# Row statistics, normalised rows and softmax scaling on VectorE: one tile of a chunk to a quarter of a slot

## Chip, core and metric

The kernel runs on one core of a Trainium2 chip. The metric is the device time of one execution in microseconds (us). TensorE does the matrix products and transposes, VectorE, ScalarE and POOL the elementwise work and reductions, and SyncE (SP) issues most of the transfers. The engines run their own instructions in order and meet at semaphores.

## The reference, cut to what matters

`x` has 2048 tokens of width 256, `ctx` has 1601. Layer 0 is a cross attention with 16 heads of width 16, then a mixture of 8 experts (the best one is taken); layer 1 is an attention over a masked window of 256 context rows, then a routing of every token to 64 slots, whose state is updated once from all tokens.

```python
x = x + xcond0(layernorm(x), ctx, ctx)          # 16 heads, softmax over 1601 keys, plus Wo
x = x + experts(layernorm(x))                   # router: softmax, top 1 of 8; y * weight
x = x + tanh(cat([align @ enc, n]) @ W_c.T)     # n = layernorm(x); align = softmax(mask(n W_a enc)) * gauss
x = x + slots(layernorm(x))                     # h = gelu(n w1); logits = h w2; alpha = softmax of the top 8 of 64;
                                                # slot update from alpha^T n over ALL tokens; out = alpha @ values
def layernorm(x): return (x - mean(x)) / sqrt(var(x) + 1e-5)
```

(The sums with `x` and the layer norms stand around the layers in the whole program; the lines above are shortened.)

## The kernel before

The tokens are four chunks of 512, and a chunk is four tiles of 128 rows (`TT` = 4). The main loop takes a chunk's attention in 52 slots: four head groups times 13 blocks of 128 keys. A slot has four quarters, one for each head of the group, so a chunk has 208 quarters.

In each quarter TensorE makes one score product (line 1189, two buffers, `ps_e`), ScalarE takes its exponential (line 750), and at the end of a slot TensorE multiplies the probabilities of the slot before with the values (line 985). The softmax needs the maximum of each row of scores beforehand. So TensorE also makes the scores of the next head group a first time (line 901, `max_unit`) in pieces of 401 columns into a ring of three buffers (`RING` = 3), and VectorE reduces each piece to a maximum (line 1335, `take_max`). There are 1, 2, 1, 1 of these products in the four quarters of most slots. Product u waits until piece u - 3 has been reduced. In the last third of chunk 3 there are no more such products, since there is no chunk after it.

All that follows the attention of chunk c, from the output projection to the slots, runs in the quarters of chunk c + 1: the functions `behind(c)` of TensorE, VectorE, ScalarE and POOL. They are generators. A `yield q` tells that what follows is due in quarter q, and each engine's `go_on` runs what is due after its own attention work of that quarter (on VectorE after the maxima of the quarter and, in the first quarter of a slot's third key block, after `normalise`). The jobs of the last chunk run after the main loop without quarters, in the same order on each engine.

The quarter of each job is worked out by `places` from the table `JOBS` (name, job it follows, least distance in quarters, quarters that it holds its buffer). The TensorE jobs share two banks in turn; a job needs the bank of the one but one before it to be read out. The order of the banks counts two fixed kinds of job too, the turned attention output ("o", quarters 6, 58, 110, 162) and the turned maxima ("m", 45, 97, 149, 201), so a job can be pushed past them. `AT[name]` is the quarter.

The layer norms go as follows (t1 before the experts, t2 before the window, t3 before the slots). VectorE computes the statistics of each tile (`bn_stats`, line 1417) and their aggregate (`bn_aggr`, line 1421). POOL adds epsilon and takes the power -0.5 (lines 597 and 599, `rsqrt`). VectorE waits for it (`rstd_ready`), writes four tiles of `xn` (line 1327, `normal`), and TensorE transposes them (`turned`, jobs t1a, t1b and so on; line 1030), waiting for `xn_ready` at t1a, t2a and t3a. ScalarE copies the transposes to `xnT` (line 760).

In the window softmax, VectorE adds the mask, takes the row maximum (line 1490), negates it (line 1492), ScalarE takes the exponentials of the four tiles with their sums (line 793), VectorE divides (`reciprocal`, then line 1504 for each tile) and TensorE transposes (aTa, aTb). In the slots, VectorE computes `alpha` (lines 1528 to 1556) from the logits, and TensorE multiplies it with `xn` (job slots, line 1171).

SP stores `x` after the third sum (`x3`) and loads the next chunk's `x` into the same tile once the third `xn` of the chunk is written.

Of the kernel before, what the change touches and what calls it, by code (L numbers as in the profile page):

```python
# [12 lines left out]
ALU = mybir.AluOpType  # L13
# [4 lines left out]
T, D = 2048, 256  # L18
# [4 lines left out]
NC = T // CT  # L23
TT = CT // P
# [5 lines left out]
NE = 2 * TT * NX // 4  # L30
# [91 lines left out]
def units_at(k, h):  # L122
# [5 lines left out]
O_AT = [HG * (ST * g + 1) + 2 for g in range(NG)]  # L128
M_AT = [HG * k + 1 for k in range(SLOTS) if max_end(k - 1) is not None]

JOBS = [("ota", None, 10, 3), ("otb", "ota", 2, 3), ("y0", "otb", 3, 3), ("y1", "y0", 2, 3), ("t1a", "y1", 11, 3),
        ("t1b", "t1a", 2, 3), ("router", "t1b", 3, 2), ("e0", "router", 5, 6)]
JOBS += [(f"e{i}", f"e{i - 1}", 4, 6) for i in range(1, 4)] + [("gateT", "e3", 3, 3), ("e4", "gateT", 1, 6)]
JOBS += [(f"e{i}", f"e{i - 1}", 4, 6) for i in range(5, NE)]
JOBS += [("gb0", f"e{NE - 1}", 4, 4), ("gb1", "gb0", 2, 4), ("t2a", "gb1", 11, 3), ("t2b", "t2a", 2, 3),
         ("score0", "t2b", 3, 3), ("score1", "score0", 2, 3), ("aTa", "score1", 13, 3), ("aTb", "aTa", 2, 3),
         ("z0", "aTb", 3, 9), ("z1", "z0", 8, 9), ("t3a", "z1", 20, 3), ("t3b", "t3a", 2, 3), ("h", "t3b", 3, 5),
         ("logits", "h", 6, 2), ("slots", "logits", 14, 6), ("alphaT", "slots", 4, 3)]


def places():

    fixed = sorted([(q, q + 3) for q in O_AT] + [(q, q + 2) for q in M_AT])
    ring, at = [(0, 0), (0, 0)], {}
    for name, after, lag, hold in JOBS:
        q = at[after] + lag if after else lag
        while True:
            while fixed and fixed[0][0] < q:
                ring.append(fixed.pop(0))
            q = max(q, ring[-2][1])  # L150
            if not fixed or fixed[0][0] >= q and ring[-1][1] <= fixed[0][0]:
                break
            q = max(q, fixed[0][0] + 1)
        at[name] = q
        ring.append((q, q + hold))
    return at


AT = places()
# [38 lines left out]
def build(nc, io):  # L198
    with ExitStack() as ctx:
        def sb(name, shape, dt=F32):  # L200
            return ctx.enter_context(nc.sbuf_tensor(name, shape, dt))
# [4 lines left out]
        def sem(name):  # L206
            return ctx.enter_context(nc.semaphore(name))
# [9 lines left out]
        xres = sb("xres", [P, TT, D])  # L217
# [18 lines left out]
        alphaT = alphaT_raw[0:NS + 1, :]  # L236
        xa = sb("xa", [P, TT, D])
# [6 lines left out]
        xb = sb("xb", [P, TT, D])  # L244
        xn = sb("xn", [P, TT, D + 1])
# [47 lines left out]
        mv = sb("mv", [P, TT, 2])  # L293
        var_e = sb("var_e", [P, TT])
        rstd = sb("rstd", [P, TT])
# [18 lines left out]
        at = [0]  # L314
# [51 lines left out]
        s = {n: sem(n) for n in names}  # L366
# [10 lines left out]
        def bank(job, c):  # L377
            return ps_m[:, RING + JOB[job, c] % 2, :]
# [284 lines left out]
        def _(act):  # L663
# [79 lines left out]
            for _, now in BESIDE:  # L743
                step(*now)
# [508 lines left out]
        def _(dve):  # L1253
# [67 lines left out]
                    last = dve.bn_aggr(mv[:, t, :], bst[:, t, :])  # L1321
                last.then_inc(s["var_ready"], 1)

            def normal(src, n):
                dve.wait_ge(s["rstd_ready"], n)
                for t in range(TT):
                    last = dve.tensor_scalar(xn[:, t, 0:D], src[:, t, :], mv[:, t, 0:1], rstd[:, t:t + 1],  # L1327
                                             ALU.subtract, ALU.mult)
                last.then_inc(s["xn_ready"], 1)

            def take_max(u, n1):
                t, h, q = u // (QUARTERS * HG), (u // QUARTERS) % HG, u % QUARTERS
                dve.wait_ge(s["max_ready"], UNITS * n1 + u + 1)
# [77 lines left out]
            def spread_stats(src, at):  # L1411

                dve.drain()
                for t in range(TT):
                    if t % 2 == 0:
                        yield at + t // 2
                    dve.bn_stats(bst[:, t, :], src[:, t, :])
                yield at + 2
                dve.drain()
                for t in range(TT):  # L1420
                    last = dve.bn_aggr(mv[:, t, :], bst[:, t, :])  # L1421
                last.then_inc(s["var_ready"], 1)

            def behind(c):

# [5 lines left out]
                yield AT["y1"] + 3  # L1431
                yield from spread_stats(xa, AT["y1"] + 3)
                yield AT["t1a"] - 4
                normal(xa, NC + 3 * c + 1)

                yield AT["router"] + 1
                wait_filled(dve, "router", c)
# [27 lines left out]
                for i in range(NE):  # L1465
                    t, j = i // 4, i % 4
                    for e in (2 * j, 2 * j + 1):
                        yield AT[f"e{i}"] + 4 + e % 2
                        dve.drain()
                        if e % 2 == 0:  # L1470
                            wait_filled(dve, f"e{i}", c)
                        last = dve.scalar_tensor_tensor(out=xb[:, t, :], in0=bank(f"e{i}", c)[:, D * (e % 2):D * (e % 2) + D],  # L1472
                                                        scalar=hot8[:, t, e:e + 1], in1=(xb if e else xa)[:, t, :],
                                                        op0=ALU.mult, op1=ALU.add)
# [4 lines left out]
                    take_sum(xb[:, 2 * i:2 * i + 2, :], xb[:, 2 * i:2 * i + 2, :], f"gb{i}", c)  # L1479
                yield from spread_stats(xb, AT["gb1"] + 4)  # L1480
                yield AT["t2a"] - 4
                normal(xb, NC + 3 * c + 2)

                for i in range(2):
                    yield AT[f"score{i}"] + 2
                    at = slice(2 * i, 2 * i + 2)
# [12 lines left out]
                dve.reciprocal(st4[:, 6, :], rowsum[:])  # L1499
                dve.drain()  # L1500
                for t in range(TT):
                    if t == 2:
                        yield AT["score1"] + 9
                    last = dve.tensor_scalar(work[:, t, :], work2[:, t, :], st4[:, 6, t:t + 1], None, ALU.mult)
                last.then_inc(s["a_ready"], 1)
                if c == NC - 1:
# [13 lines left out]
                                           work[:, 2 * i:2 * i + 2, :], ALU.add)  # L1520
                x3.then_inc(s["x3_ready"], 1)
                yield from spread_stats(xres, AT["z1"] + 11)
                yield AT["t3a"] - 3
                normal(xres, NC + 3 * c + 3)

                yield AT["logits"] + 1
                wait_filled(dve, "logits", c)
# [165 lines left out]
```

## Time and profile before

| what | before |
|---|---|
| median of 3 runs | 1118.73 us (1114.81 to 1122.76) |
| the profiled execution | 1120.53 us |
| its span, first to last instruction | 1118.8 us |
| TensorE busy | 1008.3 us, 90% |
| VectorE busy | 742.0 us, 66% |
| ScalarE busy | 573.4 us, 51% |
| POOL busy | 62.3 us, 6% |
| mean granted TensorE clock | 0.960 of full speed |

The span is 1.7 us shorter than the execution's own time. Busy TensorE (PE) is not TensorE at its peak, since matmuls are pipelined and their ends are modelled. Lines such as L1335 are lines of the kernel. Quarters are found in the trace by counting the products of line 1189, of which each quarter has one: chunk 1 begins at 264.88 us, and its quarter 20 at 286.23.

### The profile page before, as it was taken

Reading aid. Unit: us, or ns where it says so; the run is one execution under the profiler, and the core shown is the slowest. Engines: PE = TensorE matmul, PEld = TensorE weight load, DVE = VectorE, ACT = ScalarE, POOL = GpSimd, SP = SyncE. Lnnn points to the kernel's source line nnn. Section 1 sums busy time; section 2 is a strip of 40 time slices with the busy share of each in tenths; the row PEclk is TensorE's granted clock in tenths of the full one; section 3 lists DMA queues with packets and bytes.
Section 4 is the critical chain, followed back from the end, with each engine's and each line's share of the span. In section 5 each row is a group of like instructions: output and inputs, shape, how many; then the busy total and the mean of one; then the engine's idle time right before and its main releaser. Section 6 shows DMA issues by size and latency. Waiting matters only on the chain.

```text
span 1118.8 us, 13600 instructions
## 1 busy us (share of the span) xinstructions
PE 1008.3 (90%) x4825; PEld 403.5 (36%) x4825; DVE 742.0 (66%) x1681; ACT 573.4 (51%) x1056; POOL 62.3 (6%) x85
## 2 busy tenths in 40 slices
PE   6788999999889989989989989898999989889887
PEld 3443223223333334423333334323333333244634
DVE  4578877877667777776667776777677672125343
ACT  3455676676445456665445456655444467620220
POOL 3341000000000000000000000001000000000000
PEclk9899999999999989999899999999999899699998
DMA  7925600001000000001000000010000001040022
GB/s 183 193 70 95 121 11 15 6 10 34 1 16 1 15 0 13 4 6 48 1 15 1 16 1 15 1 53 1 15 1 1 1 1 39 1 119 0 1 95 75
DMA packets 33773, 36.06 MB, mean 32 GB/s; under 512 B 6639, under 2 KB 30365, under 8 KB 33445
## 3 DMA queue, kind: packets, MB, share of 16 engines
q1 hardware_dynamic: 32384, 34.04, 12.1%
q10 hardware_dynamic: 1242, 0.90, 0.6%
q8 instruction: 38, 0.62, 0.2%
q0 software_dynamic: 80, 0.26, 0.1%
q14 instruction: 29, 0.24, 0.1%
HBM read 21.42 MB, written 7.35 MB: 26 GB/s over the span
## 4 chain that ended last, share of the span: by engine, by line
issue 52%; PE 28%; DVE 9%; DMA 4%; ACT 2%; POOL 2%; DVEq 2%; SPq 1%; POOLq 0%; ACTq 0%
PE ps_e L1189 7%; PE ps_o L985 7%; PE ps_m L901 6%; DVE mx L1335 4%; PE ps_e L861 2%; DMA xres<-in_x 1%; SPq L471 1%; POOL rstd L599 1%; DMA q_stack<-probs 1%; POOL xres L650 1%; ACT probs L750 1%; DVE xn L1327 1%; PE ps_m L1133 1%; PE ps_m L1136 1%; PE ps_m L1248 1%
## 5 line engine op out<-in xcount | busy, mean ns | idle before, releaser
L1335 DVE TENSOR_REDUCE mx<-ps_m 128x1 f32<-128x401 f32 x1024 | 539.4, 569 | 212.3 <-PE ps_m L901 204.1
L750 ACT ACTIVATE probs<-ps_e 128x512 f32<-128x512 f32 (+1 forms) x832 | 472.2, 597 | 362.3 <-PE ps_e L1189 360.9
L901 PE MATMUL ps_m<-k_stack,q_stack 99*128 99x401 bf16 x1024 | 319.1, 343 | 34.4 <-DVE mx L1335 29.7
L1189 PE MATMUL ps_e<-q_stack,k_stack 101*128 101x512 bf16 (+1 forms) x832 | 329.2, 398 | 11.8 <-ACT probs L750 9.1
L985 PE MATMUL ps_o<-probs,v_heads 128*32 128x512 f32 (+1 forms) x1664 | 231.7, 630 | 0.0
L1189 PEld LDWEIGHTS ps_e<-q_stack,k_stack 101*128 101x128 bf16 (+1 forms) x832 | 82.5, 100 | 314.0 <-ACT probs L750 215.5
L901 PEld LDWEIGHTS ps_m<-k_stack,q_stack 99*128 99x128 bf16 x1024 | 102.3, 100 | 150.8 <-DVE mx L1335 90.9
L1083 PE MATMUL ps_m<-expert_w,xnT 128*128 128x512 f32 x256 | 129.1, 605 | 16.3 <-DVE xb L1472 16.3
L1472 DVE SCALAR_TENSOR_TENSOR xb<-ps_m,hot,xb 128x256 f32<-128x256 f32 x112 | 54.2, 484 | 18.1 <-PE ps_m L1083 8.9
L1083 PEld LDWEIGHTS ps_m<-expert_w,xnT 128*128 128x128 f32 x256 | 46.7, 193 | 47.4 <-DVE xb L1472 24.7
L985 PEld LDWEIGHTS ps_o<-probs,v_heads 128*32 128x32 f32 (+1 forms) x1664 | 33.4, 110 | 66.6 <-issue 56.9
L597 POOL TENSOR_TENSOR var_e<-mv,eps 128x4 f32<-128x4 f32 x16 | 3.2, 199 | 679.3 <-DVE mv L1421 676.2
L760 ACT COPY xnT<-ps_m 128x512 f32<-128x512 f32 x24 | 13.8, 587 | 46.5 <-PE ps_m L1030 46.5
L1005 PE MATMUL ps_m<-wc,ident 128*128 128x512 f32 x64 | 30.9, 624 | 0.8 <-ACT alphaT L819 0.8
L650 POOL TENSOR_TENSOR xres<-xres,bo 128x1024 f32<-128x1024 f32 x4 | 9.4, 2350 | 266.9 <-DMA xres<-in_x 266.9
L861 PE MATMUL ps_e<-xnT,expert_w 128*128 128x512 f32 x32 | 18.8, 677 | 4.4 <-issue 3.1
L1133 PE MATMUL ps_m<-win_v,work 128*128 128x256 f32 x64 | 19.6, 399 | 2.3 <-ACT work L760 2.3
L1519 DVE TENSOR_TENSOR xres<-xb,work 128x512 f32<-128x512 f32 x8 | 5.5, 687 | 22.4 <-ACT work L803 22.4
L1136 PE MATMUL ps_m<-wc,xnT 128*128 128x256 f32 x64 | 19.3, 395 | 0.0
L1030 PE MATMUL ps_m<-ident,xn 128*128 128x128 f32 x96 | 17.8, 283 | 1.3 <-DVE xn L1327 1.2
L677 ACT ACTIVATE work<-ps_e,cond 128x512 f32<-128x512 f32 (+1 forms) x11 | 7.2, 653 | 22.2 <-PE ps_e L861 22.2
L1040 PE MATMUL ps_m<-win_k,xnT 128*128 128x256 f32 x64 | 16.2, 383 | 2.2 <-issue 1.4
(241 smaller groups left out, 636.9 us busy)
## 6 DMA issues: line engine op xcount, KB each, us to landing
q_stack<-q_parts SPq DMA_DIRECT2D x78, 64.0 KB, 2.6
expert_w<-in_expert_wT SPq DMA_DIRECT2D x2, 1024.0 KB, 13.2
xres<-in_x SPq DMA_DIRECT2D x4, 512.0 KB, 3.8
x<-xres SPq DMA_DIRECT2D x4, 512.0 KB, 3.2
probs<-x SPq DMA_DIRECT2D x1, 2048.0 KB, 8.4
out<-probs SPq DMA_DIRECT2D x4, 512.0 KB, 3.0
k_stack<-alphaT SPq DMA_DIRECT2D x10, 200.1 KB, 7.7
probs<-in_ctxT SPq DMA_DIRECT2D x3, 512.0 KB, 7.8
```

The source lines that it names most:

```text
L650: pool.tensor_tensor(xres[:], xres[:], bo0[:].unsqueeze(1).broadcast_to((P, TT, D)), ALU.add)\
L750: act.activation(probs[0:n, k % 2, h, :], ps_e[h % 2][0:n, :], ACT.Exp).then_inc(s["exp_done"], 1)
L861: mm = pe.matmul(ps_e[b % 2][:, 0:n], wqkv[:, w, k, P * m:P * m + P], src[:, k, at_col:at_col + n], start=(k == 0), stop=(k == KT - 1))
L901: pe.matmul(ps_m[:, (UNITS * n1 + u) % RING, 0:SPLIT], qst[0:MAX_ROW, g, h, P * t:P * t + P], kst[0:MAX_ROW, HG * g + h, QUARTER_START[q]: ...
L985: mm = pe.matmul(ps_o[32 * h:32 * h + 32, :], v_sb[0:n, st, HG * g + h, :], probs[0:n, k % 2, h, :], start=(st == 0), stop=(st == ST - 1))
L1005: pe.matmul(out, ident[:], wc[:, 0:KT, :], start=True, stop=True)
L1083: mm = pe.matmul(bank(name, c), xnT[:, k, P * t:P * t + P], expert_w[:, k, CT * j:CT * j + CT], start=(k == 0), stop=(k == KT - 1))
L1133: pe.matmul(o, aT[:, k, tok:tok + P], win_v[:, k, :], start=(k == 0), stop=False)
L1136: mm = pe.matmul(o, xnT[:, k, tok:tok + P], wc[:, KT + k, :], start=False, stop=(k == KT - 1))
L1189: pe.matmul(ps_e[h % 2][0:n, :], kst[0:ROWS, HG * g + h, P * st:P * st + n], qst[0:ROWS, g, h, :], start=True, stop=True).then_inc(s["qk_r ...
L1335: dve.tensor_reduce(mx[:, q, col:col + 1], ps_m[:, (UNITS * n1 + u) % RING, 0:SPLIT], AX.X, ALU.max)\
L1472: last = dve.scalar_tensor_tensor(out=xb[:, t, :], in0=bank(f"e{i}", c)[:, D * (e % 2):D * (e % 2) + D], scalar=hot8[:, t, e:e + 1], in1=( ...
```

## The change

The statistics of tile t are due in quarter `at + t` (before: two tiles in `at`, two in `at + 1`), the aggregate in `at + 4` (before `at + 2`). `normal` is replaced by `spread_normal`: it waits for `rstd` once, then writes the tile t in quarter `at + t`, where all four were written in one quarter. The softmax scaling of tile t is due in `AT["score1"] + 8 + t` (before two in + 8, two in + 9). In `JOBS`, t1a and t2a follow their predecessors by 12 quarters instead of 11, slots follows logits by 12 instead of 14, and alphaT follows slots by 3 instead of 4. For t3 the first tile comes at `AT["t3a"] - 4` instead of - 3.

```diff
-JOBS = [("ota", None, 10, 3), ("otb", "ota", 2, 3), ("y0", "otb", 3, 3), ("y1", "y0", 2, 3), ("t1a", "y1", 11, 3),
+JOBS = [("ota", None, 10, 3), ("otb", "ota", 2, 3), ("y0", "otb", 3, 3), ("y1", "y0", 2, 3), ("t1a", "y1", 12, 3),
...
-JOBS += [("gb0", f"e{NE - 1}", 4, 4), ("gb1", "gb0", 2, 4), ("t2a", "gb1", 11, 3), ("t2b", "t2a", 2, 3),
+JOBS += [("gb0", f"e{NE - 1}", 4, 4), ("gb1", "gb0", 2, 4), ("t2a", "gb1", 12, 3), ("t2b", "t2a", 2, 3),
...
-         ("logits", "h", 6, 2), ("slots", "logits", 14, 6), ("alphaT", "slots", 4, 3)]
+         ("logits", "h", 6, 2), ("slots", "logits", 12, 6), ("alphaT", "slots", 3, 3)]
...
-            def normal(src, n):
-                dve.wait_ge(s["rstd_ready"], n)
-                for t in range(TT):
-                    last = dve.tensor_scalar(xn[:, t, 0:D], src[:, t, :], mv[:, t, 0:1], rstd[:, t:t + 1],
-                                             ALU.subtract, ALU.mult)
-                last.then_inc(s["xn_ready"], 1)
...
                 for t in range(TT):
-                    if t % 2 == 0:
-                        yield at + t // 2
+                    yield at + t
                     dve.bn_stats(bst[:, t, :], src[:, t, :])
-                yield at + 2
+                yield at + 4
                 dve.drain()
                 for t in range(TT):
                     last = dve.bn_aggr(mv[:, t, :], bst[:, t, :])
                 last.then_inc(s["var_ready"], 1)
+
+            def spread_normal(src, n, at):
+
+                dve.wait_ge(s["rstd_ready"], n)
+                for t in range(TT):
+                    yield at + t
+                    last = dve.tensor_scalar(xn[:, t, 0:D], src[:, t, :], mv[:, t, 0:1], rstd[:, t:t + 1],
+                                             ALU.subtract, ALU.mult)
+                last.then_inc(s["xn_ready"], 1)
...
                 yield AT["t1a"] - 4
-                normal(xa, NC + 3 * c + 1)
+                yield from spread_normal(xa, NC + 3 * c + 1, AT["t1a"] - 4)
...
                 yield AT["t2a"] - 4
-                normal(xb, NC + 3 * c + 2)
+                yield from spread_normal(xb, NC + 3 * c + 2, AT["t2a"] - 4)
...
                 for t in range(TT):
-                    if t == 2:
-                        yield AT["score1"] + 9
+                    yield AT["score1"] + 8 + t
                     last = dve.tensor_scalar(work[:, t, :], work2[:, t, :], st4[:, 6, t:t + 1], None, ALU.mult)
...
-                yield AT["t3a"] - 3
-                normal(xres, NC + 3 * c + 3)
+                yield AT["t3a"] - 4
+                yield from spread_normal(xres, NC + 3 * c + 3, AT["t3a"] - 4)
```

Worked out by `places` from the two tables, the quarters are:

| job | before | after | | job | before | after |
|---|---|---|---|---|---|---|
| ota, otb, y0, y1 | 10, 12, 15, 17 | the same | | t2a, t2b | 125, 127 | 127, 129 |
| t1a, t1b | 28, 30 | 29, 31 | | score0, score1 | 130, 132 | 132, 134 |
| router | 33 | 34 | | aTa, aTb | 145, 147 | 147, 150 |
| e0, e1, e2, e3 | 38, 42, 48, 52 | 39, 43, 49, 53 | | z0, z1 | 150, 158 | 153, 161 |
| gateT, e4 | 55, 58 | 59, 61 | | t3a, t3b | 178, 180 | 181, 183 |
| e5 to e12, every 4 | 64 to 92 | 65 to 93 | | h, logits | 183, 189 | 186, 192 |
| e13, e14, e15 | 98, 102, 106 | 99, 103, 107 | | slots | 203 | 204 |
| gb0, gb1 | 112, 114 | 113, 115 | | alphaT | 207 | 207 |

Due quarters on VectorE at the three layer norms (first and last statistics, aggregate, first and last tile, then TensorE's transposes): t1 before 20, 21, 22, 24, 24, 28 and after 20, 23, 24, 25, 28, 29; t2 before 118, 119, 120, 121, 121, 125 and after 119, 122, 123, 123, 126, 127; t3 before 169, 170, 171, 175, 175, 178 and after 172, 175, 176, 177, 180, 181. Beside that the gateT job now comes after the "o" job at 58, and aTb after the "m" job at 149, which changes which bank they take.

## Rows read from the trace of the kernel before

**Rows 1.** The page, part 1: busy us, share of the span, instructions

```profile
PE 1008.3 (90%) x4825; PEld 403.5 (36%) x4825; DVE 742.0 (66%) x1681; ACT 573.4 (51%) x1056; POOL 62.3 (6%) x85
```

**Rows 2.** Busy us (instructions) by chunk (1 and 3): engines, clock, DMA, GB/s

```profile
264.88:505.32 240.44, 219.61 (x1125) 85.05 (x1121) 176.02 (x392) 133.04 (x243) 5.98 (x7) 0.98 0.04 11
...
748.44:982.14 233.70, 212.34 (x1034) 78.40 (x1030) 135.35 (x310) 131.15 (x241) 8.32 (x8) 0.93 0.04 12
```

**Rows 3.** TensorE's waits in chunk 1: us in total, times, longest

```profile
PE ps_m L901 <- DVE mx L1335: 9.8, 18, 1.8
PE ps_m L1083 <- DVE xb L1472: 5.1, 4, 1.6
PE ps_e L1189 <- ACT probs L750: 1.8, 5, 0.8
PE ps_m L1040 <- issue: 0.9, 2, 0.5
...
PE ps_m L1161 <- ACT hT L811: 0.5, 1, 0.5
```

**Rows 4.** Timeline around t1 in chunk 1: start us, us, what [idle before, releaser]

```profile
286.23 0.39 PE L1189 MATMUL ps_e<-q_stack,k_stack 101*128 101x512 bf16 x1
...
292.28 1.38 DVE L1327 TENSOR_SCALAR xn<-xa,mv,rstd 128x256 f32<-128x256 f32 x4 [0.53 <-POOL rstd L599]
...
296.88 0.38 PE L1189 MATMUL ps_e<-q_stack,k_stack 101*128 101x512 bf16 x1
```

**Rows 5.** TensorE's waits for maxima in chunk 1: around t1, t2, t3

```profile
PE ps_m L901 <- DVE mx L1335: 2.7, 3, 1.8
...
PE ps_m L901 <- DVE mx L1335: 2.0, 4, 0.8
...
PE ps_m L901 <- DVE mx L1335: 1.8, 4, 0.5
```

**Rows 6.** Timeline around t2 in chunk 1, VectorE and TensorE

```profile
409.54 0.38 DVE L1421 BATCH_NORM_AGGREGATE mv<-bst 128x2 f32<-128x6 f32 x4
...
411.39 1.38 DVE L1327 TENSOR_SCALAR xn<-xb,mv,rstd 128x256 f32<-128x256 f32 x4 [0.52 <-POOL rstd L599]
...
412.68 3.46 DVE L1335 TENSOR_REDUCE mx<-ps_m 128x1 f32<-128x401 f32 x7
...
414.59 0.39 PE L1030 MATMUL ps_m<-ident,xn 128*128 128x128 f32 x2
414.81 0.38 PE L1189 MATMUL ps_e<-q_stack,k_stack 101*128 101x512 bf16 x1
...
415.20 0.38 PE L1030 MATMUL ps_m<-ident,xn 128*128 128x128 f32 x2
...
416.51 0.39 PE L1189 MATMUL ps_e<-q_stack,k_stack 101*128 101x512 bf16 x1
```

**Rows 7.** Timeline around gb0 in chunk 1, TensorE and VectorE

```profile
396.08 0.67 PE L1099 MATMUL ps_m<-expert_b_tiles,gateT 32*128 32x256 f32 x2 [0.47 <-DVE xb L1472]
396.52 0.25 DVE L1400 RECIPROCAL z_inv<-ps_m 128x16 f32<-128x16 f32 x1
...
396.85 0.42 DVE L1403 TENSOR_TENSOR attn_chunk<-ps_m,z_inv 128x256 f32<-128x256 f32 x1
```

**Rows 8.** Timeline around the score scaling in chunk 1, TensorE

```profile
431.60 0.39 PE L1189 MATMUL ps_e<-q_stack,k_stack 101*128 101x512 bf16 x1 [0.46 <-ACT probs L750]
```

**Rows 9.** Timeline around slots in chunk 1, VectorE and TensorE

```profile
497.14 0.43 DVE L1556 TENSOR_TENSOR work<-work,st 128x256 f32<-128x256 f32 x1
...
498.38 0.65 PE L1171 MATMUL ps_m<-xn,work 128*64 128x257 f32 x2
```

**Rows 10.** Stretches around t1's gap in chunks 1 and 2, as above

```profile
290.00:298.00 8.00, 5.84 (x38) 2.61 (x34) 6.86 (x19) 4.02 (x8) 1.22 (x2) 1.00 0.00 0
530.00:538.00 8.00, 5.84 (x28) 1.89 (x25) 5.82 (x17) 2.94 (x6) 1.22 (x2) 0.84 0.00 0
```

**Rows 11.** VectorE: max line, chunk 1; busy us, mean ns | idle

```profile
L1335 DVE TENSOR_REDUCE mx<-ps_m 128x1 f32<-128x401 f32 x256 | 136.8, 569 | 56.6 <-PE ps_m L901 54.7
```

## The prediction

> **What bounds the kernel.** I read the page's busy table first: TensorE is busy 1008.3 of the 1118.8 us [rows 1]. That alone does not say that it works all the time, so I cut the main loop at its four chunks [rows 2]. Chunk 1, with all jobs of chunk 0 beside its own attention, takes 240.4 us. Its list of TensorE's waits [rows 3] gives 9.8 us on VectorE's maxima, 1.8 us on ScalarE's exponentials and small ones on single jobs. So TensorE sets the pace, VectorE holds it up in bursts, and the change is about these bursts. It acts in chunks 1 to 3. Chunk 0 has no such jobs, and after chunk 3 there is no slot left to spread over: there the same instructions stand in the same order on each engine, so I add nothing for the end.
>
> How a burst costs TensorE time is seen in the stretch around t1a in chunk 1 [rows 4]. VectorE waits 0.53 us for POOL's rstd, then writes four tiles of xn in one go (1.38 us). Behind them stand the maxima. TensorE may be three products ahead of the maxima taken (its three buffers of scores), and so its next product stands still for 1.8 us. The stretches around the three layer norms hold 2.7 us (t1), 2.0 us (t2) and 1.8 us (t3) of the 9.8 us [rows 5]; most of the rest belongs to scores and logits, which the change does not split.
>
> **What the change moves.** No instruction is added or removed: statistics, xn tiles and scalings are the same in number and shape. Three things move. (1) Four statistics, four xn tiles and four scalings go one to a quarter. (2) The distances shrink: the last xn tile comes one quarter ahead of the transposes that read it, where all four came four quarters ahead (three for t3), and the aggregate, which POOL waits for, comes one quarter ahead of the first xn tile at t1 and t3, and in the same quarter at t2. (3) All jobs from t1a on fall one to three quarters later, so they meet other neighbours in their slot; the last margins shrink: slots follows logits by 12 quarters and not 14, while its alpha is still written in quarter logits + 11.
>
> SP's and POOL's queues move with it. x3 is stored, and the next x loaded, three quarters later; that x is needed only at y0 of the next chunk, 40 quarters on, so I add nothing. If that cover were gone, y0 would wait for the load.
>
> **t2, step by step.** The aggregate ends at 409.92 and the first xn tile starts at 411.39 [rows 6]: 1.47 us through POOL, of which two maxima now hide 0.95. In the new order nothing stands between them, so the whole 1.47 us is bare. Four more maxima now come ahead of the aggregate, at 0.48 us each (seven in 3.46 us): it ends at about 409.92 + 1.9 = 411.8. From there VectorE's queue is: 1.47 us wait, tile, max, tile, two maxima, tile, max, tile. Tiles are 0.33 us apart, maxima 0.48. The max of quarter 124 is out 1.47 + 0.33 + 0.57 = 2.37 us after the aggregate; the product of quarter 126 needs its buffer, and TensorE would be there at about 411.75. It stands until 414.2, a single gap of 2.4 us. The last tile is out 1.47 + 3 x 0.33 + 4 x 0.48 + 0.41 = 4.8 us after it, at 416.6. In quarter 127 TensorE now waits for just this tile, does two transposes (0.22) and the slot's probability product (1.1), and begins quarter 128 at 417.9. Before, it began it at 416.51 with four more transposes done (0.44 us). So t2 costs 1.4 + 0.44 = **+1.8 us** a chunk. Bounds: 0 if VectorE has no backlog there, +3.6 if the wait costs in full beside today's 2.0.
>
> **t1 and t3.** At t1 two maxima still stand between aggregate and tile, so POOL's wait stays at 0.5 us. The four tiles end at 293.66 now [rows 4], with the maxima up to quarter 24 ahead of them. In the new order those of quarters 25 to 28, five more, stand ahead of the last tile: it ends at 293.66 + 5 x 0.48 = 296.1. TensorE waits for it in quarter 29, does two transposes and begins quarter 30 at 296.36 and not at 296.88, with two transposes fewer done (0.22): **-0.3 us** a chunk. The burst is gone, but the wait for xn has taken its place. Bounds: -2.7 (all of today's waits, [rows 5]) and +1. At t3 POOL's wait, hidden now, shows 0.6 us, and the same reckoning gives **+0.35 us**, from -1.8 to +1.5. Only chunks 1 and 2 count: chunk 3 has no maxima left in its last third (310 VectorE instructions against 392, [rows 2]).
>
> **The jobs in their new neighbourhoods.** None of these stands in the trace in its new place, so each takes the nearest row, zero on the other side unless said.
> - gb0 needs the bank that e15's second gate product frees. Before, e15 was done at quarter 111 and gb0 waited 0.47 us. Now it is done at quarter 112, where VectorE first normalises the attention of a head group (0.25 + 0.42 us) and takes a max [rows 7]: about **+1.0 us**.
> - The other bank waits of the e jobs (5.1 us a chunk today, [rows 3]) keep their length within 0.2 us each: e2 -0.2, e13 +0.15, the pair gateT and e4 +0.15. Sum **+0.1**, from -1 to +1.
> - Score scaling. ScalarE's row exponentials now delay one score product by 0.46 us [rows 8]; the other is hidden by the probability product that TensorE does just then. In the new phase ScalarE gets the negated maximum as TensorE starts a slot, with no probability product to hide behind: two products wait, 0.7 and 1.0 us, and the maxima cost as much as now. **+1.3 us**. score0, now at the start of a slot, no longer waits for its xnT copy: **-0.5**, about the wait that L1040 shows twice.
> - aTb now shares its bank with aTa and waits for ScalarE's copy (0.5), z0 waits 0.2 more: **+0.7**.
> - h and logits: the two table loads around gelu begin in a quarter that hides 0.5 us less than today, when logits waits 0.5 us [rows 3]: **+0.5**.
> - slots: alpha ends at 497.57 and its first reader starts at 498.38 in quarter 203 [rows 9], not waiting. Now three quarters of margin become one, and elg's product, its sum, the row maximum's copy, a max, reciprocal and alpha (some 2.9 us) stand ahead: a wait of 2.5 us, less the 1 us that maxima cost there today: **+1.5**, chunks 1 and 2.
>
> **Sum.** Chunks 1 to 3: -0.3 + 1.8 + 1.0 + 0.1 + 1.3 - 0.5 + 0.7 + 0.5 = 4.6, times 3 is 13.8. Chunks 1 and 2: (0.35 + 1.5) x 2 = 3.7. Together +17.5 us. The profiled execution took 1120.5 us, so 1138 by its own time. The median of the runs is 1118.7, 0.16% lower: **1136 us**.
>
> **The clock, and a rule weighed.** In chunk 2 the granted clock is 0.84 over the 8 us that hold t1's gap, 1.00 in chunk 1 at the same place [rows 10], with TensorE busy 5.84 us in both: a spell at 1.2 in place of 2.4 GHz that comes in some chunks and costs some 0.16 x 8 = 1.3 us. A gap like it can bring one, so five larger gaps (t2 three times, slots twice) could cost 5 x 1.3 = 6.5 us; I count none in the sum.
> The Trainium skill, "TensorE: Matmul & The Clock Gate", section on HAM oscillation, says that waits between groups of matmuls bring the clock down to half and that it must be earned back: it speaks against a change that gathers small waits into one of 2.4 us. By that rule the sum would be the third rival's; the trace agrees in chunk 2 and not in chunk 1.
>
> **The rivals.**
> - *Faster*: VectorE has room enough in each slot, so the spread tiles never stop TensorE and xn is there in time. It would save all burst waits of [rows 5], (2.7 + 2.0) x 3 + 1.8 x 2 = 17.7 us: 1118.7 - 17.7 = 1101. It decides from where VectorE's work up to the last tile fits into TensorE's own: at t1 that is 296.1 - 286.2 = 9.9 us against 7.5 (quarters 20 to 29 took 296.88 - 286.23 = 10.65 us, less 2.7 of waits and 0.44 of transposes, [rows 4, 5]), and the 1.47 us through POOL speaks against it most. For it: VectorE waits 54.7 of 240 us of chunk 1 for products, in its max line [rows 11].
> - *No difference*: TensorE's new neighbours cost nothing, as the waits in one quarter let VectorE or ScalarE catch up for the next. Then only t1, t2 and t3 are left, (1.8 - 0.3) x 3 + 0.35 x 2 = 5.2: 1124. For it: these prices come from replaying single places, and no row of before shows one of them.
> - *The clock falls* after each of the five new gaps: 1136 + 6.5 = 1143. For it chunk 2, against it chunk 1 [rows 10].
>
> **How the numbers follow.** My forecast 0.58, no difference 0.24, faster 0.10, falling clock 0.08. A measurement of this kernel tells about 1% from no change, 11 us. Slower by over 1%, above 1130, takes the forecast's 0.58 less 0.04 for its lower edge, the clock's 0.08 and 0.02 of the second rival: 0.64. Within 1% takes the rest of these two, 0.26; faster 0.10. The range leaves out the faster rival and the upper half of the last: 1113 to 1145; the forecast's own is 1128 to 1143.
>
> **What would show it.** Right: in chunks 1 to 3 a single wait of the max product on VectorE of over 2 us near quarter 126, xn's first tile of t2 waiting 1.4 us for POOL, transposes of xn waiting for VectorE at t1a, t2a and t3a, L1171 waiting for alpha in chunks 1 and 2, gb0 waiting over 1 us, chunk 0 and the end unchanged. Wrong: POOL's wait hidden at t2, transposes that never wait, or chunk 1 at or below 240 us.

## The result: 2.2% slower, and the profile after

The changed kernel takes 1139.69 us (median of 6 runs, 1138.6 to 1151.43) against 1120.74 us for the kernel before beside it; the ratio is 1.0216, 95% interval 1.018 to 1.0252. The forecast was 1136 us in 1113 to 1145. The profiled execution took 1139.54 us, with a span of 1137.9 us and a mean granted clock of 0.958 (before 1118.8 and 0.960).

First the page's part 1 of the kernel after, to be read against [rows 1]: the same 13600 instructions, TensorE busy 4.8 us longer in a span 19.1 us longer.

```profile
PE 1013.1 (89%) x4825; PEld 403.2 (35%) x4825; DVE 740.9 (65%) x1681; ACT 567.0 (50%) x1056; POOL 62.3 (5%) x85
```

Then the busy time of each engine in chunks 1, 2 and 3 of the kernel after, with their sum (the stretch and its length; PE, PEld, DVE, ACT, POOL busy; granted clock; DMA share and GB/s). It answers [rows 2]:

```profile
266.34:515.88 249.54, 225.05 (x1125) 86.03 (x1121) 175.85 (x392) 130.93 (x243) 5.98 (x7) 0.96 0.04 12
515.88:765.02 249.14, 225.00 (x1126) 85.92 (x1122) 175.84 (x392) 130.97 (x243) 5.99 (x7) 0.96 0.04 11
765.02:1000.47 235.45, 210.63 (x1032) 78.41 (x1028) 134.98 (x310) 129.12 (x241) 8.34 (x8) 0.95 0.03 10
sum 734.13, PE 660.68 PEld 250.36 DVE 486.67 ACT 391.03 POOL 20.30; mean PE 220.23 PEld 83.45 DVE 162.22 ACT 130.34 POOL 6.77
```

The same view of the kernel before, its sum over the three chunks:

```profile
sum 717.26, PE 654.78 PEld 249.50 DVE 487.82 ACT 397.58 POOL 20.28; mean PE 218.26 PEld 83.17 DVE 162.61 ACT 132.53 POOL 6.76
```

A chunk's length less TensorE's busy time is what TensorE stood still. It was 717.26 - 654.78 = 62.5 us and is 734.13 - 660.68 = 73.5 us: **11.0 us of new waits**. The same products also took 660.68 - 654.78 = **5.9 us longer**. Most of that is the clock: by the trace's clock records the stretches at 1.2 GHz add up to 58.0 us in the three chunks before and 64.9 after, and half of the difference, 3.4 us, is lost; the other 2.5 us were not split. Together 16.9 of the 19.1 us; chunk 0 is as long as before (167.0 against 166.8 us), the start and the end are 1.3 and 0.8 us longer.

TensorE's waits in chunk 1 after the change (line, what it waited for, us in total, times, longest), against [rows 3]:

```profile
PE ps_m L901 <- DVE mx L1328: 6.5, 13, 2.1
PE ps_e L1189 <- ACT probs L750: 3.0, 6, 0.9
PE ps_m L1030 <- DVE xn L1421: 2.7, 3, 1.1
PE ps_m L1083 <- DVE xb L1473: 2.5, 2, 1.6
PE ps_m L1171 <- DVE work L1556: 1.8, 1, 1.8
PE ps_m L1099 <- DVE xb L1473: 1.4, 1, 1.4
PE ps_m L1090 <- DVE xb L1473: 1.3, 1, 1.3
...
PE ps_m L1030 <- DVE work L1504: 0.4, 1, 0.4
```

The waits for maxima did fall, from 9.8 to 6.5 us: the bursts are gone. What has come in their place is three waits of transposes for the last tile of xn (2.7 us), one of slots for alpha (1.8), a longer one at gb0 (1.4 for 0.5), and more waits for ScalarE (3.0 for 1.8).

The clock shows in the stretches around gb0 and behind t2 (same columns as the chunks). Before:

```profile
399.00:412.00 13.00, 11.85 (x49) 3.11 (x49) 8.33 (x22) 5.20 (x10) 1.21 (x2) 0.74 0.00 0
...
417.00:425.00 8.00, 7.53 (x41) 4.45 (x40) 4.92 (x9) 3.92 (x7) 0.00 (x0) 1.00 0.01 2
```

After:

```profile
400.00:413.00 13.00, 12.95 (x42) 3.49 (x41) 6.96 (x14) 5.06 (x10) 0.00 (x0) 0.61 0.00 0
417.00:425.00 8.00, 6.13 (x22) 2.10 (x23) 4.34 (x11) 1.69 (x4) 0.00 (x0) 0.57 0.00 0
```

A granted clock of 1.00 is 2.4 GHz, 0.5 is 1.2 GHz; 0.61 and 0.57 are stretches mostly at the lower level. Behind gb0 TensorE lost 13 x (1 - 0.74) = 3.4 us before and 5.1 us now, with hardly any idle time inside the stretch (12.95 of 13 us busy); gb0's wait of 1.43 us lies just ahead of it. Behind t2's gap it lost nothing before and 8 x 0.43 = 3.4 us now. Both come in all three chunks (behind t2 from 418, 667 and 916 us on). Not all went one way: of the kernel before's own low stretches, those behind t1's gap in chunks 2 and 3 are gone [rows 10], and one of 17 us late in chunk 3 has shrunk to 3.

**Waits and clock apart.** A profile is one execution, and the clock differs between executions of one kernel. Each run has a span and a mean granted clock; the time lost to the clock is (1 - clock) x span. Over all runs below, each taken against the mean of its own kernel, the span moves by 0.73 us for each us lost. Taking that off gives a span at equal clock, in which runs of one kernel agree within 0.5 to 1.5 us (standard deviation). "Idle" is the three chunks' TensorE idle time in the profiled execution, worked out as above.

| kernel | ratio to before (95%) | idle | lost to the clock | span at equal clock |
|---|---|---|---|---|
| before | 1 | 62.5 | 40.3 | 1089.1 |
| after (jobs moved, work spread) | 1.0216 (1.018 to 1.0252) | 73.5 | 51.9 | 1102.9 |
| e1: jobs moved alone | 1.0139 (1.0106 to 1.0173) | 62.7 | 57.6 | 1091.9 |
| e8: work spread alone | 1.0144 (1.0105 to 1.0183) | 68.9 | 51.2 | 1097.1 |
| e2: after, t2's statistics earlier | 1.0216 (1.0184 to 1.0249) | 70.1 | 51.7 | 1103.3 |
| e3: after, quick rstd | 1.0149 (1.012 to 1.0177) | 68.4 | 51.0 | 1097.2 |
| e4: after, t2's gap filled | 1.0233 (1.0204 to 1.0261) | 65.0 | 52.4 | 1104.5 |
| e5: after, gb0's gap filled | 1.0207 (1.0164 to 1.0251) | 69.4 | 45.7 | 1108.2 |
| e6: after, gb with 128 rows | 1.0101 (1.0063 to 1.0139) | 74.1 | 37.9 | 1101.5 |
| e7: before, gb with 128 rows | 0.9913 (0.9884 to 0.9942) | 64.3 | 31.0 | 1086.3 |
| e9: e7 with jobs moved | 0.9946 (0.9915 to 0.9977) | 66.3 | 32.5 | 1089.3 |
| e10: e7, t1a one quarter later | 0.9818 (0.9782 to 0.9853) | 58.9 | 24.4 | 1081.0 |
| e11: e7, t1a two quarters later | 0.9846 (0.981 to 0.9882) | 60.6 | 26.6 | 1082.8 |
| e12: e11 with t1 spread | 0.9831 (0.9796 to 0.9866) | 60.6 | 21.6 | 1083.9 |

By this reckoning the change's 22 us of mean span are 13.8 us that stay at equal clock (1102.9 - 1089.1), which are put down to waits, and 0.73 x (51.9 - 40.3) = 8.5 us of clock. The clock's part is worked out from scatter within each kernel, not seen in one trace; that it holds between kernels is assumed. The profiled pair has it lower, 11.0 us of idle time and 3.4 to 5.9 of clock, and so have most pairs below: the equal-clock figures are good to a few us.

### The profile page after: what moved, and what is told of

Same layout as the page of the kernel before. It is cut to its first block, busy times and chain, and to the rows that moved or that the text cites. A ratio compares the mean times of both kernels' runs of the same rounds, so it can differ in the third digit from the quotient of the medians.

```text
span 1137.9 us, 13600 instructions
## 1 busy us (share of the span) xinstructions
PE 1013.1 (89%) x4825; PEld 403.2 (35%) x4825; DVE 740.9 (65%) x1681; ACT 567.0 (50%) x1056; POOL 62.3 (5%) x85
## 4 chain that ended last, share of the span: by engine, by line
issue 63%; PE 21%; DVE 6%; DMA 4%; ACT 2%; POOL 2%; SPq 1%; DVEq 1%; POOLq 0%; ACTq 0%
PE ps_e L1189 5%; PE ps_m L901 5%; PE ps_o L985 5%; DVE mx L1328 2%; PE ps_e L861 2%; DMA xres<-in_x 1%; POOL rstd L599 1%; DMA q_stack<-probs 1%; SPq L471 1%; POOL xres L650 1%; PE ps_m L1248 1%; DMA probs<-in_ctxT 1%; ACT probs L750 1%; DMA x<-xres 1%; PE ps_m L1005 1%
## 5 line engine op out<-in xcount | busy, mean ns | idle before, releaser
L750 ACT ACTIVATE probs<-ps_e 128x512 f32<-128x512 f32 (+1 forms) x832 | 464.7, 596 | 376.7 <-PE ps_e L1189 375.4
L1030 PEld LDWEIGHTS ps_m<-ident,xn 128*128 128x128 f32 x96 | 13.1, 153 | 17.8 <-DVE xn L1421 12.7
```

The lines of the kernel that those rows point to most:

```text
L750: act.activation(probs[0:n, k % 2, h, :], ps_e[h % 2][0:n, :], ACT.Exp).then_inc(s["exp_done"], 1)
L1030: mm = pe.transpose(bank(name, c)[:, P * t:P * t + P], src[:, t, P * k:P * k + P], ident[:])
```

## The experiments

### The change in two halves: e1 and e8

e1 is the kernel before with the new distances of the jobs and nothing else:

```diff
-("t1a", "y1", 11, 3)
+("t1a", "y1", 12, 3)
-("t2a", "gb1", 11, 3)
+("t2a", "gb1", 12, 3)
-("slots", "logits", 14, 6), ("alphaT", "slots", 4, 3)
+("slots", "logits", 12, 6), ("alphaT", "slots", 3, 3)
```

> The kernel before with the changed JOBS table alone: all jobs stand in the quarters of the changed kernel, but statistics, rows and scaling keep their old bunches of two and four. Theory A (the jobs' new neighbours cost some waits, the spread's bare wait for POOL and the clock that falls behind it cost the rest): gb0 waits 1.4 us and slots 1.2 us longer than before, t2's longest wait for a max stays under 1 us, no low clock at quarter 127; +7 us, 1124 to 1131. Rival B (the moved jobs are all of it): 1137 to 1141. Rival D (the spread is all of it): 1117 to 1123.

e8 is the other half, every other hunk of the change on the old distances.

> The kernel before with the one-tile-to-a-quarter code alone, the distances of the jobs as before the change (the other half of the first experiment). Statistics and xn of t1 and t2 now lie one quarter closer. Theory A (moved jobs bring most of the lost clock, the spread most of the waits): slots and gb0 wait as before the change (no 1.8 us for alpha, 0.5 us for gb0), t1 and t2 each show a bare wait of 1.4 us for POOL and a single max wait of 2 us, the waits of a chunk are 24 to 26 us, the clock is that of before, 1128 to 1134. Rival: the closer distances at t1 and t2 cost more than the moved jobs did, waits of 28 us a chunk, 1140 to 1148.

Measured: 1136.03 us for e1 (1.0139) and 1136.14 us for e8 (1.0144). Two halves with one price, but not of one kind. TensorE's waits in chunk 1 of e1, and then of e8:

```profile
PE ps_m L901 <- DVE mx L1335: 5.8, 14, 1.5
...
PE ps_m L1171 <- DVE work L1556: 1.8, 1, 1.8
PE ps_m L1099 <- DVE xb L1472: 1.4, 1, 1.4
```

```profile
PE ps_m L901 <- DVE mx L1328: 10.1, 14, 2.3
PE ps_m L1083 <- DVE xb L1473: 5.1, 4, 1.6
PE ps_m L1030 <- DVE xn L1421: 2.0, 2, 1.3
...
PE ps_m L1099 <- DVE xb L1473: 0.5, 1, 0.5
```

e1 lies between its theories (1124 to 1131 and 1137 to 1141), and two signs of theory A failed. The product of quarter 126 waits 1.48 us, and the clock falls behind t2 in all three chunks, for 3.4 us each:

```profile
419.23 0.34 PE L901 MATMUL ps_m<-k_stack,q_stack 99*128 99x401 bf16 x1 [1.48 <-DVE mx L1335]
```

So a gap of this kind comes with the moved jobs alone; the spread alone has one too (2.23 us, in quarter 125 of e8's chunk 1). e8 lies above its theory (1128 to 1134) and below the rival. Its clock is not that of before (51.2 us lost, before 40.3), which its theory had wrong.

The moved jobs alone take the waits for maxima from 9.8 [rows 3] to 5.8 us, with every burst still in place: at t1, where one quarter more lies between the burst and its reader, three waits of 2.7 us [rows 5] become four of 1.2. They pay at slots and gb0 and end at before's idle time, 62.7 us; what they cost is the clock. The spread alone has the old waits at slots and gb0 and none of that relief: maxima still cost 10.1 us, the longest single wait is 2.3 and not 1.8 us, and transposes wait for xn on top. At equal clock it costs 8.0 us, the moved jobs 2.8, both together 13.8. The halves need not add up: on the old distances the spread of e8 has one quarter less between statistics and transposes at t1 and t2 than in the change, and POOL's answer is laid bare at t1 too (the 2.3 us). So the gain that the change has in its maxima comes from its distances, not from the spreading; its waits for xn come from the spreading.

### t2: POOL's answer in the bare, e2, e3 and e4

The chain that the forecast replayed from [rows 6], in the kernel after (chunk 1, VectorE, POOL and TensorE; start us, us, line, what, idle time before it):

```profile
414.98 0.38 DVE L1413 BATCH_NORM_AGGREGATE mv<-bst 128x2 f32<-128x6 f32 x4
...
415.78 1.01 POOL L599 TENSOR_TENSOR rstd<-var_e,neg_half 128x4 f32<-128x4 f32 x1
416.82 0.41 DVE L1421 TENSOR_SCALAR xn<-xb,mv,rstd 128x256 f32<-128x256 f32 x1 [1.46 <-POOL rstd L599]
...
417.77 0.40 PE L901 MATMUL ps_m<-k_stack,q_stack 99*128 99x401 bf16 x1 [2.13 <-DVE mx L1328]
```

From aggregate to tile nothing stands on VectorE for 1.46 us, and TensorE's product of quarter 126 waits 2.13 us in one piece; the transposes then wait 1.09 us for the last tile. e2 starts the statistics of t2 a quarter earlier:

```diff
-                yield from spread_stats(xb, AT["gb1"] + 4)
+                yield from spread_stats(xb, AT["gb1"] + 3)
```

> The changed kernel with the statistics of t2 one quarter earlier, so that the two maxima of a quarter stand again between the aggregate and the first row tile. Theory A: the wait for POOL at t2 falls from 1.46 us to about 0.5, the product of quarter 126 waits 1.2 and not 2.1 us; if the low clock at quarter 127 comes from that gap it goes too. 1128 to 1137. Rival B (moved jobs): no change, 1138 to 1141.

The same stretch in e2, VectorE's first tile and TensorE's product of quarter 126:

```profile
413.19 0.41 DVE L1421 TENSOR_SCALAR xn<-xb,mv,rstd 128x256 f32<-128x256 f32 x1 [1.01 <-POOL rstd L599]
...
414.14 0.34 PE L901 MATMUL ps_m<-k_stack,q_stack 99*128 99x401 bf16 x1 [1.32 <-DVE mx L1328]
```

One max now hides 0.45 us of the round trip and the gap falls to 1.32 us; the transposes wait 1.26 us instead of 1.09, and another max 0.24. All waits at t2 together fall only from 3.2 to 2.8 us in chunk 1, because the transposes wait for the last tile anyway. Idle time in the profiled execution falls 3.4 us, busy time grows 4.7: ratio 1.0216, no gain. That is the rival's outcome, but not its reason, for the moved jobs are not all of it (e8). e3 makes POOL's answer itself short; its expectation says what it leaves out:

```diff
-neg_half[:], ALU.pow)
+neg_half[:], ALU.mult if n > NC else ALU.pow)
```

> The changed kernel, with POOL multiplying where it takes the power in the loop's layer norms (left out: the power, so rstd has another value). The step on POOL falls from 1.01 to about 0.2 us. Theory A: VectorE's wait at t2 falls from 1.46 to about 0.65 us, at t1 and t3 from 0.5 to nothing; 4 to 5 us of waits go, and the low clock at quarter 127 perhaps: 1127 to 1135. Rival (VectorE's backlog alone holds TensorE, POOL's wait is inside it): 1138 to 1141.

The same stretch in e3:

```profile
418.15 0.20 POOL L599 TENSOR_TENSOR rstd<-var_e,neg_half 128x4 f32<-128x4 f32 x1
418.39 0.41 DVE L1421 TENSOR_SCALAR xn<-xb,mv,rstd 128x256 f32<-128x256 f32 x1 [0.66 <-POOL rstd L599]
419.34 0.34 PE L901 MATMUL ps_m<-k_stack,q_stack 99*128 99x401 bf16 x1 [1.32 <-DVE mx L1328]
```

POOL takes 0.20 in place of 1.01 us, VectorE's bare wait is 0.66, and a wait of 0.46 us for maxima at t1 and t3 is gone too. The signs of theory A are there, and the time (1135.75 us) is just above its range. The ratio falls from 1.0216 to 1.0149, 7.5 us; at equal clock it is 5.7 us. TensorE's waits at t1, t2 and t3 fall by 3.9 us over the three chunks, the idle time by 5.1. The 5.7 us also hold what the last chunk's three layer norms gain behind the main loop, where the kernel before could gain it too. So the round trip through POOL, laid bare, carries 4 to 6 of the 14 us. At t2 it is about 0.5 us a chunk, no more than at t1; 2.8 us of waits stay there as in e2 (1.32, 0.24 and 1.20 for xn): the last tile is one quarter ahead of its reader.

e4 leaves the order as it is and gives TensorE something to do in the gap, three products with the identity that nobody reads:

```diff
+                if c < NC - 1:
+                    yield AT["t2a"] - 2
+                    bank_free(pe, "t2a", c)
+                    keep_warm(2, bank("t2a", c))
                 yield AT["t2a"]
+                if c < NC - 1:
+                    keep_warm(1, bank("t2a", c))
```

> The changed kernel with three products of the identity added on TensorE in chunks 1 to 3, two ahead of quarter 126 and one ahead of the transposes of quarter 127, into the bank that the transposes then overwrite: about 2 us of work where TensorE waits 3.2 us. Theory A (the clock falls for the gap): the waits shrink by the filling, the end of the stretch stays, and the low clock at quarter 127 goes: 1129 to 1135. Rival C (the clock falls for the jobs ahead of it, gb0 and gb1): low clock as before the filling, 1139 to 1146.

Its stretches around gb0 and around t2 in chunk 1 (columns as above), and late in the chunk:

```profile
396.00:409.00 13.00, 13.00 (x42) 3.54 (x41) 6.77 (x13) 4.18 (x8) 0.00 (x0) 0.61 0.00 0
410.00:421.00 11.00, 9.80 (x49) 3.79 (x49) 7.87 (x22) 4.70 (x10) 1.21 (x2) 1.00 0.01 1
490.00:510.00 20.00, 16.32 (x70) 5.02 (x71) 13.49 (x42) 10.97 (x21) 0.00 (x0) 0.83 0.06 16
```

Behind t2 the clock stays at 1.00 in all three chunks, where it was 0.57: the waits there had brought it down. But the time is 1145.15 us (1.0233), in the range of the rival, whose reason (low clock behind t2 as before the filling) is wrong. The loss to the clock over all runs is the same, 52.4 us: in the profiled execution low stretches now lie at quarters 143, 194 and 204, where the kernel after has few or none, and the one at gb0 is 3.4 us longer in two chunks. Where one gap was filled the low clock went and came elsewhere; it was not given back. Why it came there is not shown.
The Trainium skill, "TensorE: Matmul & The Clock Gate", section on HAM oscillation, has it that waits between groups of products bring the clock down; the waits of its case are for transfers and longer than any here. At t2 the trace agrees that waits do it (0.57 with the gap of 2.13 us, 1.00 with it filled).

### gb0: what brings the clock down there, e5, e6, e7 and e9

Every kernel so far runs at 1.2 GHz from quarter 114 or 115 on, before or after the change. Two suspects: the wait at gb0 just ahead, and the four products of gb0 and gb1 themselves (eight MATMUL instructions in the trace), which contract (sum over) only 32 rows. e5 fills the wait with three identity products, e6 and e7 give the products 128 rows, those from 32 on zero, in the kernel after and before:

```diff
+                    if i == 0 and c < NC - 1:
+                        pe.wait_ge(s["exp_done"], HG * SLOTS * (c + 1) + AT["gb0"])
+                        keep_warm(3, ps_e[(AT["gb0"] + 1) % 2][:, 0:CT])
```

```diff
-        eb = sb("expert_b_tiles", [TT * NX, TT, D])
+        eb = sb("expert_b_tiles", [P, TT, D])
-        gateT = sb("gateT", [TT * NX, P])
+        gateT = sb("gateT", [P, P])
+            pool.memset(gateT[:], 0.0)
-taken(act.copy(gateT[:], bank("gateT", c)[0:TT * NX, 0:P]), "gateT", c)
+taken(act.copy(gateT[0:TT * NX, :], bank("gateT", c)[0:TT * NX, 0:P]), "gateT", c)
```

> The changed kernel with three 512-column identity products on TensorE in quarter 113 of chunks 1 to 3, in the stretch in which it otherwise stands 1.43 us for gb0's bank; they write a score buffer that ScalarE has just emptied, and no result changes. Theory A (this wait is what lengthens the stretch at 1.2 GHz that begins two quarters later, 8.5 to 9 us against 5.4 to 6.5 us before the change): that stretch shrinks to 6 us or vanishes, 1.5 to 4 us less a chunk, 1128 to 1135 in all. Theory B (a stretch that is filled only moves the low clock to another place): the stretch at quarter 115 may shrink, others come, and the time stays at 1138 to 1144.

> The changed kernel with the gate-by-bias products gb0 and gb1 contracting 128 rows in place of 32, the rows from 32 on being zero; nothing else moves. Theory C (these eight small products right where the clock falls are the cause of the low stretch from quarter 115 on): the stretch goes in chunks 1 to 3, some 4 us a chunk, 1126 to 1130. Theory A or B: it stays 8 to 10 us long from quarter 115 on, 1138 to 1142.

> The kernel before with the same 128-row gb0 and gb1. Theory C: its low stretch from quarter 115 on (5.4 to 6.5 us) goes, some 3 us a chunk, 1109 to 1113. Theory A or B: no change, 1117 to 1123.

Measured 1143.58, 1129.93 and 1111.92 us. The stretch from gb0 on in e5, then in e6 (with the one behind t2), then in e7:

```profile
396.00:409.00 13.00, 12.82 (x55) 4.30 (x54) 8.65 (x19) 5.78 (x11) 0.00 (x0) 1.00 0.00 0
```

```profile
393.00:406.00 13.00, 11.31 (x63) 4.30 (x61) 10.47 (x23) 6.98 (x13) 0.00 (x0) 1.00 0.00 0
411.00:419.00 8.00, 6.15 (x22) 2.28 (x23) 4.35 (x10) 1.95 (x4) 0.00 (x0) 0.58 0.00 0
```

```profile
399.00:412.00 13.00, 11.05 (x63) 4.08 (x59) 11.34 (x28) 6.84 (x12) 0.94 (x2) 1.00 0.00 0
```

The 128-row products cost nothing and the low stretch is gone from all three chunks of both kernels: 9.8 us less after the change and 8.6 before, as theory C had it. In the profiled execution of e7 nothing came in its place (30.7 us at 1.2 GHz in the three chunks, before 58.0); in that of e6 other stretches did (58.0 against 64.9), so that its 9.8 us rest on the runs and not on this stretch alone. In e6 gb0's wait is still there, in the timeline:

```profile
397.19 0.67 PE L1100 MATMUL ps_m<-expert_b_tiles,gateT 128*128 128x256 f32 x2 [1.44 <-DVE xb L1474]
```

So this wait alone doesn't bring the clock down, nor do the thin products alone: in e5 they follow no wait and the clock stays at 1.00. In these kernels it took both.
That section of the Trainium skill speaks of waits alone and not of the rows that a product contracts; by the trace the wait alone is not enough here (1.00 behind a wait of 1.44 us).
e5 gained nothing for two reasons. Its three fillers took 2.84 us in a hole of 1.43, and at equal clock it is 5.3 us slower than the kernel after; and, as its theory B had it, other low stretches came (61.4 us in the three chunks of the profiled execution, none of them at gb0).

The change's price is not in this place, though: with 128 rows the kernel after still stands 18.0 us behind the kernel before (1129.93 - 1111.92), as without (19.0). e9 splits it, moved jobs alone on e7:

> The kernel before with 128-row gb0 and gb1 and the moved jobs alone, nothing spread. It stands against the kernel before and the changed kernel with the same 128 rows (1111.9 and 1129.9 us). Theory A (what the moved jobs cost alone was the long stretch at 1.2 GHz from quarter 114 on, since their waits were no longer than before): 1114 to 1118. Rival (their lost clock lies in many places and the moved jobs cost the same 15 us with or without it): 1124 to 1130.

Measured 1113.68 us, just under theory A's range, 1.8 above e7, in place of the 16 that e1 stood above the kernel before (1136.03 against 1119.91 beside it). The intervals overlap, so with 128 rows the moved jobs cost nothing that was measured: their price alone went with the thin products. The stretch at gb0 is not all of it. In the profiled execution of e1 it had grown from 20.5 to 37.5 us over the three chunks, 8.5 us of lost clock; the other low stretches had grown too (37.5 to 47.8 us) and are 30.7 in e9, and no run shows why these went with it. What remains, 16.3 us between e9 and e6, is the spread's: at equal clock 12.2 us (7.8 of idle time in the profiled pair), and 0.73 x (37.9 - 32.5) = 3.9 us of clock, of which the 0.58 behind t2 is in sight above.

### Room: e10, e11 and e12

If the spread's price is its margins, the same spread with more room should cost nothing. And if the relief in e1 is the distance at t1, it can be had without moving the other jobs. All three are e7 with one place changed; e0 follows the router sooner, so that everything from e0 on stands where it stood before:

```diff
-("t1a", "y1", 11, 3)
+("t1a", "y1", 12, 3)
-("e0", "router", 5, 6)
+("e0", "router", 4, 6)
```

That is e10; e11 has 13 and 3. e12 is e11 with t1's statistics spread as in the change, and its tiles from `AT["t1a"] - 5` on, so that the last stands two quarters ahead of the transposes.

> The kernel before with 128-row gb0 and gb1, t1a, t1b and router one quarter later and e0 four and not five quarters behind the router: all jobs from e0 on stand where they stood before the change, nothing is spread. Theory A (one quarter more between the burst of xn and its reader is what shortened t1's waits from 2.7 to 1.2 us with the moved jobs, and the low clock that sometimes follows them goes too): 4 to 8 us under 1111.9, 1104 to 1108. Rival (another wait takes its place): 1110 to 1114.

> As the run before, with t1a two quarters later and e0 three behind the router. Theory A: no better than one quarter later, 1104 to 1109. Rival: the router's result now comes late for gateT, 1110 to 1114.

> As the run before, with t1's statistics and xn one tile to a quarter, the last tile two quarters ahead of its reader: the spread where it has room, and nothing else spread. Theory A (the spread costs only by its distances: POOL's answer in the bare and the last tile one quarter ahead): no transpose waits for xn, t1's waits are 0.5 to 1.2 us a chunk, and the time is within 3 us of the run before. Rival (spreading costs by itself, as maxima are held up in more quarters): t1 waits 2 us and more, 4 to 8 us slower than the run before.

Measured 1100.6, 1103.86 and 1101.17 us. TensorE's waits for maxima in chunk 1 of e10, and of e12:

```profile
PE ps_m L902 <- DVE mx L1336: 8.4, 18, 0.8
```

```profile
PE ps_m L902 <- DVE mx L1336: 8.7, 19, 0.8
```

The longest is 0.8 us in both, and no transpose of t1 waits in either. e10 has the lowest median, 1.8% under the kernel before, and e11 and e12 lie within its interval. It gained 11.3 us on e7, more than its theory had: t1's wait of 1.83 us is gone (1.2 us in four pieces are left), and with it the low stretch at quarter 27 that e7 has in all three chunks; the loss to the clock falls from 31.0 to 24.4 us over the runs. In the profiled executions the three chunks of e10 are only 3.0 us shorter than those of e7, as e10's has a low stretch of 17 us late in chunk 3; 5.6 us more lie behind the main loop, where nothing was changed. So how much of the clock's part belongs to t1 is open. Given two quarters, spreading costs nothing (1101.17 against 1103.86, intervals overlapping), and gains nothing that was measured against the burst with one quarter more. It was tried with room at t1 alone; t2, t3 and the scalings were not.

## Why the prediction held, and where it did not

Per chunk, TensorE's waits at each place in chunk 1 (the waits for maxima and of the job there, summed from the trace) against the forecast's terms:

| place | forecast | waits before, after | measured |
|---|---|---|---|
| t1 | -0.3 | 2.7, 1.9 | -0.8 |
| t2 | +1.8 | 2.1, 3.2 | +1.1 |
| gb0 | +1.0 | 0.5, 1.4 | +1.0 |
| other banks of the e jobs | +0.1 | 5.1, 4.6 | -0.5 |
| score scaling | +1.3 | 1.4, 1.8 | +0.4 |
| score0 | -0.5 | 0.5, 0 | -0.5 |
| aT transposes and z0 | +0.7 | 0.4, 1.8 | +1.3 |
| h, logits | +0.5 | 1.9, 1.9 | 0 |
| t3 (chunks 1 and 2) | +0.35 | 1.8, 1.9 | +0.1 |
| slots (chunks 1 and 2) | +1.5 | 2.4, 3.6 | +1.2 |

- **The mechanism was right for the waits.** What the text asked to be seen is there: one wait of 2.13 us at quarter 126, xn's first tile 1.46 us behind POOL, transposes waiting at t1a, t2a and t3a, L1171 waiting 1.8 us in chunks 1 and 2, gb0 1.43 us for the 0.47 of [rows 7], chunk 0 unchanged, the end 0.8 us longer. At t2 the forecast put the gap at 2.4 us and the round trip at 1.47. But e1 has 1.48 us of that gap with nothing spread, and e2 shows that most of t2's price is the last tile's late end and not the bare round trip.
- **The waits were over-sized.** The sum gave 17.5 us, the profiled executions show 11.0. Scaling, t2, the e jobs' banks and h with logits were the terms (0.9, 0.7, 0.6 and 0.5 us a chunk too much). The two products at the scaling do wait, for 0.49 and 0.90 us (forecast 0.7 and 1.0), but the maxima around them wait less (0.96 us before, 0.43 after); that VectorE caught up while they waited is likely and not shown. At h and logits the waits are what they had been, 1.9 us.
- **A place was missed.** In aTa's quarter the max product waits 0.50 us and aTa's transposes 0.40 us for the last scaled tile, where moved jobs and spread scaling meet: in e1 the max product waits 0.23 us and aTa's transposes not at all, in e8 neither waits. The forecast looked at aTb and z0 only.
- **The clock was the step that failed.** "I count none in the sum": it is 3.4 to 5.9 us in the profiled pair and 8.5 us over all runs. The third rival had the cause, a gap that brings the clock down, and for t2 it was so in all three chunks, although the section of the Trainium skill that the forecast leant on has longer waits than the 2.4 us; but its price, 1.3 us a gap from [rows 10], is 3.4 us there, slots' gaps brought no such stretch, and the 1.7 us more at gb0 was nobody's term. Too much waiting (17.5 us for 11.0) and no clock cancelled: 1136 against 1139.7 is in part luck, two errors of 3 to 8 us with opposite signs.
- **The faster rival failed where it was said to.** It decided on whether VectorE's work up to the last tile fits. e12 shows that it does with the reader two quarters behind the last tile, and then the spread is free, but not a gain.

## What to carry over

Spreading a burst over slots also moves its end towards its reader and lays bare what stood between its parts; give it the room first (later readers), and see whether the room alone does it. Around a change that moves waits, read the granted clock by stretch and in several executions, for it can cost as much as the waits, and a filled gap may only move it. Where the clock falls while TensorE is busy, look at what it was doing: here thin products behind a wait, made full with rows of zeros at no cost, gave 9 to 10 us back.

## What the runs showed of the hardware

- A product of 32 rows ran as long as one of 128 at the same clock (0.67 us for the first product, two MATMUL instructions, in [rows 7] and in e6), yet with a wait ahead the thin ones were followed by 1.2 GHz (granted clock 0.74 and 0.61 over 13 us) while TensorE was 91% and 99.6% busy; with 128 rows it was 1.00 behind the same wait of 1.44 us.
- The low clock is not lost in full: between executions of one kernel, 1 us of (1 - clock) x span went with 0.73 us of span. That waits which were due anyway are taken up in it is likely, not shown.
- Where the low clock was driven out of one place it could come at others: with t2's gap filled (e4) the loss over all runs was 52.4 us as against 51.9.
- POOL's rstd of 128x4 elements takes 1.01 us as a power and 0.20 us as a product, a difference that the span showed (1.0216 to 1.0149).
- One identity product of 512 columns in float32 took 0.95 us of TensorE (2.84 us for three): such a filler can be longer than the hole (1.43 us in e5).
